# Feed-forward stages of a four-block layer: other priorities and other spans in the planner that sets each engine's order

## What is computed

```python
x = x + _layernorm(attn(_layernorm(x), wq, wk, wv, wo))             # attention, 32 heads
x = x + _layernorm(ffn_lora(_layernorm(x), gate, up, down, a, b))   # silu(gate) * up, then down; 1376 hidden, rank 16
x = x + _layernorm(mixer(_layernorm(x), Win, phz, W1, W2, Wout))    # width 64, 4 layers: complex scan, small MLP
x = x + _layernorm(ffn_int4(_layernorm(x), w1, s1, w2, s2, w3, s3)) # int4 weights with scales, 1376 hidden
```

## Time and profile before

| | us |
|---|---|
| median of 3 runs (838.73 to 839.6) | 838.98 |
| the profiled execution | 840.07 |
| its span, first to last instruction | 838.3 |
| its mean granted clock, full speed being 1 | 0.967 |

### The profile page before, as it was taken

One profiled execution on the slowest core, in us unless ns is written; L12 is line 12 of the kernel. 1 busy time (PEld: TensorE's weight loads), 2 busy tenths in 40 slices (PEclk: granted clock), 3 DMA queues, 4 the chain that ended last, 5 costly groups with the idle time before them and its releaser, 6 DMA issues. The chain is left out here.

```text
span 838.3 us, 12915 instructions
## 1 busy us (share of the span) xinstructions
PE 764.3 (91%) x4483; PEld 555.4 (66%) x4483; DVE 559.1 (67%) x1189; ACT 342.9 (41%) x575; POOL 447.6 (53%) x595
## 2 busy tenths in 40 slices
PE   3999899999988987979998999998989999899995
PEld 2888655555545555758776778775778776578873
DVE  4543677777766369797948787977887977730015
ACT  5111356666666454533333434324443423233510
POOL 4343232443343235754667866847786867474732
PEclk9999899999999998999999999999899999799998
DMA  9002746555470021554673434432154423142301
GB/s 310 7 1 76 236 129 214 177 177 176 158 244 1 1 97 32 179 167 125 192 241 113 135 113 143 132 123 89 39 171 143 119 88 95 38 140 74 91 1 50
DMA packets 56945, 101.38 MB, mean 121 GB/s; under 512 B 13616, under 2 KB 17200, under 8 KB 54704
## 3 DMA queue, kind: packets, MB, share of 16 engines
q1 hardware_dynamic: 53616, 82.21, 31.9%
q0 software_dynamic: 2304, 16.78, 5.5%
q10 hardware_dynamic: 960, 1.57, 0.7%
HBM read 74.58 MB, written 27.00 MB: 121 GB/s over the span
## 5 line engine op out<-in xcount | busy, mean ns | idle before, releaser
L1509 PE MATMUL psum<-xt_hi,wgu_hi 128*128 128x512 f32 (+1 forms) x352 | 142.1, 404 | 2.5 <-POOL wd_lo L783 1.5
L1509 PE MATMUL psum<-xt_hi,wgu_lo 128*128 128x512 f32 (+1 forms) x352 | 142.0, 403 | 0.0
L1509 PE MATMUL psum<-xt_lo,wgu_hi 128*128 128x512 f32 (+1 forms) x352 | 140.5, 399 | 0.0
L783 POOL TENSOR_TENSOR wgu_lo<-raw,wgu_hi 128x512 fp32r<-128x512 f32 (+1 forms) x88 | 116.9, 1332 | 35.7 <-ACT wgu_hi L922 35.2
L1299 DVE TENSOR_REDUCE negmax<-psum 128x2 f32<-128x1024 f32 (+3 forms) x128 | 104.3, 823 | 40.0 <-PE psum L1415 38.9
L820 POOL TENSOR_SCALAR_AFFINE_SELECT probs<-probs 128x256 f32<-128x256 f32 x128 | 52.4, 409 | 121.5 <-ACT probs L979 121.1
L979 ACT ACTIVATE probs<-psum 128x1024 f32<-128x1024 f32 (+3 forms) x128 | 89.6, 710 | 52.2 <-PE psum L1612 50.1
L783 POOL TENSOR_TENSOR wd_lo<-raw,wd_hi 128x512 fp32r<-128x512 f32 (+1 forms) x44 | 59.9, 1370 | 47.6 <-ACT wd_hi L929 47.6
L922 ACT ACTIVATE wgu_hi<-raw 128x512 fp32r<-128x512 f32 (+1 forms) x88 | 54.3, 618 | 73.4 <-PE psum L1506 44.7
L1142 DVE TENSOR_TENSOR hf<-sg,psum 128x512 f32<-128x512 f32 (+1 forms) x44 | 30.1, 683 | 75.2 <-PE psum L1509 63.0
L1529 PE MATMUL psum<-wd_hi,h_hi 128*128 128x512 f32 (+1 forms) x176 | 74.0, 420 | 5.4 <-DVE y L1151 2.9
(11 more groups left out here) (209 smaller groups left out, 1583.8 us busy)
## 6 DMA issues: line engine op xcount, KB each, us to landing
raw<-full SPq DMA_DIRECT2D x60, 256.0 KB, 2.7
raw<-in_gu_t SPq DMA_DIRECT2D x40, 256.0 KB, 2.9
stage_w<-in_w SPq DMA_DIRECT2D x30, 256.0 KB, 2.9
full<-stage_w SPq DMA_DIRECT2D x30, 256.0 KB, 2.8
xt_hi<-turned POOLq DMA_DIRECT2D x7, 1024.0 KB, 5.1
xt_lo<-turned POOLq DMA_DIRECT2D x7, 1024.0 KB, 7.4
turned<-w_hi SPq DMA_DIRECT2D x52, 128.0 KB, 3.1
turned<-w_lo SPq DMA_DIRECT2D x26, 128.0 KB, 2.4
```

What stands on the lines that cost most here:

```text
L783: nc.gpsimd.tensor_tensor(lo, src, hi.bitcast(F32), ALU.subtract).then_inc(sem("w_lo"), 1)
L1509: ins = nc.tensor.matmul(bank[q % 3][0:n, :], (wgu_hi, wgu_lo)[hi_w][:, q % 4, k, 0:n], XT[hi_x][:, k, ch * 512:ch * 512 + 512], start=ite ...
```

## The change

Three things are changed; the instructions stay the same in kind and number, and no value that is computed changes.

1. The planner's choice among events that can begin at the same time. Ranks above 0 no longer count. In their place stands the length of the longest chain of events behind the event, by the planner's spans, plus a constant of the stage that the event belongs to (a table of 17 constants, `URGENT`).
2. The spans given to `put` are new for some 30 kinds of events.
3. The first product of each block and chunk, and `lora_xa`, name all four `xt_lo` tiles of their chunk as what they wait for, where they named the last one; and one of the mixer's two `gate` events names the other.

```diff
-            put("DVE", 1.15, "x_stats", s, tau, ...
+            put("DVE", 1.25, "x_stats", s, tau, ...
-                put("PE", 1.0, "xt", s, tau, ...
+                put("PE", 0.7, "xt", s, tau, ...
-            put("DVE", 1.3, "h_stats", ch, n, k, ...
+            put("DVE", 1.1, "h_stats", ch, n, k, ...
-                    put("DVE", 0.5, "carry", n, ...
+                    put("DVE", 1.4, "carry", n, ...
-                put("PE", 1.0, "wout", tau, ...
+                put("PE", 2.0, "wout", tau, ...
-                put("POOL", 1.3, "w_lo", s, ch, m, c, ...
+                put("POOL", 1.4, "w_lo", s, ch, m, c, ...
-        put("DVE", 0.9, "p_sq", ...
+        put("DVE", 2.8, "p_sq", ...
-            put("DVE", 0.78 if c < 2 else 1.4, "q_shift", m, c, ...
+            put("DVE", 0.85 if c < 2 else 1.7, "q_shift", m, c, ...
-        put("DVE", 0.5, "offsets", 0, ...
+        put("DVE", 2.0, "offsets", 0, ...
...
+        def turned_tiles(s, ch):
+            return [("xt_lo", s, TB * ch + j) for j in range(TB)]
...
-                    start = [("w_lo", s, ch, m, g), ("xt_lo", s - 1, TB * ch + TB - 1), *free] if part == 0 else []
+                    start = [("w_lo", s, ch, m, g), *turned_tiles(s - 1, ch), *free] if part == 0 else []
...
+        URGENT = {('boundary', 0, 0): -57, ('boundary', 0, 1): -81, ..., ('ffn', 3, 0): -308, ('weights', 1, 1): -463, ...}
...
+        while last_ones:
+            e = last_ones.pop()
+            to_end[e] = plan[e][1] + max((plan[e][4] + to_end[f] for f in users[e]), default=0.0)
...
-            e = min(ready, key=lambda e: (max(todo[e][0], idle[plan[e][0]]), todo[e][1], todo[e][2]))
+            e = min(ready, key=lambda e: (max(todo[e][0], idle[plan[e][0]]), min(todo[e][1], 0), -to_end[e] - URGENT.get(part_of(*e), 0), todo[e][2]))
```

More of the change, by code:

```diff
@@ L419, in weights @@
                 put("ACT", 0.65, "w_hi", s, ch, m, c, after=free + [ready], rank=2)
-                put("POOL", 1.3, "w_lo", s, ch, m, c, after=(("w_hi", s, ch, m, c),), rank=2)
+                put("POOL", 1.4, "w_lo", s, ch, m, c, after=(("w_hi", s, ch, m, c),), rank=2)
         def products(s, ch, m):
@@ L519, in sandwich @@
         put("SP", 4.5, "mixer_in", after=(("merged", NM - 1),), lag=4.0)
[L520 removed]
+        put("DVE", 3.2, "scales", after=(("side_lo", 2), ("p_sq",), ("full", 1, 0, 8)), rank=3)
         mixer(0)
@@ L524, in sandwich @@
         ffn(3, 0)
-        put("DVE", 0.5, "offsets", 0, after=[("y_rstd", 2, tau) for tau in range(TB)], rank=1)
-        put("DVE", 0.5, "offsets", 1, after=[("y_rstd", 2, tau) for tau in range(TB, NT)], rank=1)
+        put("DVE", 2.0, "offsets", 0, after=[("y_rstd", 2, tau) for tau in range(TB)], rank=1)
+        put("DVE", 2.5, "offsets", 1, after=[("y_rstd", 2, tau) for tau in range(TB, NT)], rank=1)
         ffn(3, 1)
@@ L540, in sandwich, with part_of @@
                 users[d].append(e)
+        URGENT = {('boundary', 0, 0): -57, ('boundary', 0, 1): -81, ('boundary', 1, 1): -28, ('boundary', 2, 1): 46, ('boundary', 3, 0): 59, ('boundary', 3, 1): -34,
+                  ('dequant', 0, 0): -62, ('ffn', 1, 0): -86, ('ffn', 1, 1): -52, ('ffn', 3, 0): -308, ('mixer', 0, 0): 28, ('mixer', 1, 0): 65,
+                  ('other', 0, 0): -66, ('weights', 1, 0): -241, ('weights', 1, 1): -463, ('weights', 3, 0): -305, ('weights', 3, 1): 51}
+        def part_of(what, *i):
+            if what in ("q_in", "q_shift", "q_scale", "q_keep"):
+                return "dequant", 0, 0
+            if what in ("w_in", "w_hi", "w_lo"):
+                return "weights", i[0], i[1]
+            if what in ("gate_first", "gate_up", "silu", "full", "h_hi", "h_lo", "down"):
+                return "ffn", i[0], i[1]
+            if what in ("y_stats", "y_rstd", "x_sum", "x_stats", "x_rstd", "xn", "xt", "xt_hi", "xt_mix", "xt_lo"):
+                return "boundary", i[0], i[1] // TB
+            if what in ("win", "wout"):
+                return "boundary", 1 + (what == "wout"), i[0] // TB
+            if what in ("part", "sum", "y_full"):
+                return "evict", 0, 0
+            if what in ("merged", "merge", "d_keep", "lora_xa", "lora_xh", "lora_x"):
+                return "lora", 0, 0
+            if what == "carry" or what[0:2] == "p_" or what in ("bout_hi", "bout_lo", "turns", "scales", "decay", "offsets", "out", "mixer_in") or not i or what[0:4] == "side" or what[-2:] == "wo" or what[0:2] == "o_":
+                return "other", 0, 0
+            return "mixer", i[0], 0
@@ L1476, in flow_step @@
                         after(pe, e, "side_lo", k)
-                    after(pe, e, "xt_lo", 0, TB * ch + TB - 1)
+                    for tile in turned_tiles(0, ch):
+                        after(pe, e, *tile)
                     if ch:
@@ L1496, in flow_step @@
                         if m == 0 and g == 0:
-                            after(pe, e, "xt_lo", s - 1, TB * ch + TB - 1)
+                            for tile in turned_tiles(s - 1, ch):
+                                after(pe, e, *tile)
                         if q >= 3:
```

61 lines of the change are left out of this document (33 added, 28 removed).

## The result

The changed kernel takes 818.02 us (median of 4 runs, 816.40 to 821.52) against 838.87; the ratio is 0.9755, with an interval of 0.9723 to 0.9788. The prediction was 819.5, in a range of 810 to 835. The profiled execution took 821.52, the slowest of the four, at a mean clock of 0.975 (the others 0.978 to 0.980).

What follows compares the result with a forecast made beforehand. PE, busy 764.3 of 838.3 us, bounds the kernel, so order pays only where PE waits. Savings of 2.7, 3.6, 2.8, 3.5, 2.0 and 9.2 less 4 make 19.8: 840.07 becomes 820.3, median 819.2; predicted 819.5, range 810 to 835.

Steps and rivals of the forecast that it cites:

- A: Start of ffn(1,0): lora_xa waits less as DVE work ahead of it moves behind; 2.7 us saved, ends 1.5 and 5.5.
- B: Merges in ffn(1,0): two p_low steps go behind merge 4; 3.6 us of 5.65 idle saved, ends 0 and 7.
- C: End of ffn(1,0) and way into mixer 0: h_lo, xt and win come sooner; 2.8 us saved, between 1 and 4.
- D: End of ffn(1,1): y_full ahead of the offsets ends a wait; 3.5 us saved, ends 1 and 6.4.
- E: Way into mixer 1: win, xt and h_turn of tiles 4 to 7 sooner; 2.0 us saved, ends 0 and 2.5.
- F: End of ffn(3,0): down-weight split, wout and xt sooner, half clock open; 9.2 us saved, ends 5 and 10.5.
- G: Both mixers: 84 PE steps stand sooner than their chains may allow; loss of 4 us, ends gain 3, loss 9.
- the rest: From the first product of ffn(3,1) to the last product: same work in the same order, predicted difference 0.
- rival of half the gain: Whole kernel: DVE and POOL lengths change with their neighbours, waits partly return; 10 us gained, 830 (829 median), chance 0.30.
- pot: All that a better order could give: 30.8 us of PE idle and 14.4 of lowered clock, some 45 us.
- the rival: Mixers: PE parks at side steps standing too early, blocking products behind; slower, 846 (844.5 median), chance 0.11.
- signs that the prediction named: Right: short merge waits, earlier y_full and ffn(3,1), no half clock. Wrong: mixer idle over 5 us, or half clock remaining.

Runs made afterwards that it cites:

- h1_first_part: New order up to the start of hidden tile 9 of ffn(1,0), the kernel before's order from there on; 833.59 us, ratio 0.9967.
- fix_d: Changed kernel with xt, xt_hi and xt_lo of s = 2, tile 3, moved sooner at the end of ffn(1,1); 818.05 us, ratio 0.9766.
- light_powers: Changed kernel in its order, with four of six operations of each p_low and p_high step left out; 814.19 us, ratio 0.9724.
- fix_b: Changed kernel with two DVE events moved: p_abs behind the fourth merge, the fifth merge ahead of p_low 0; 816.97 us, ratio 0.9759.
- off_only: Kernel before with one event moved, the first offsets behind the first h_centre of mixer 1; 832.06 us, ratio 0.9947.
- h2_last_part: Kernel before's order up to the start of hidden tile 9 of ffn(3,0), the new order from there on; 828.75 us, ratio 0.9925.
- fix_all: Changed kernel with the moves of fix_d and fix_b, and h_down 1 1 0 one product later; 818.92 us, ratio 0.9784.

## Why the prediction was right, and where it was not

The sum was 820.3 for the profiled execution and 819.2 for the median; the measured values are 821.5 and 818.0. It came so close because errors cancelled: the terms A to F, G and the rest are off by 2.0, 4.1, 1.2, 0.5, 2.0, 1.3, 1.4 and 1.5 us, each way. To that extent the number is luck.

The table of terms is from one execution of either kernel. Traces of other runs have one of the two orders in a stretch and give its distance again; they tell which differences are firm:

| term | old order: before; other traces | new order: after; other traces |
|---|---|---|
| A | 14.2; 14.0, 13.9 | 9.6; 8.9 to 9.5 |
| B | 101.2; 101.1, 101.1 | 101.8; 101.7 (*h1_first_part*), 98.4 (*fix_d*) |
| C | 33.9; 33.9, 33.9 | 32.3; 32.2 to 32.6 |
| D | 16.4; 16.4, 16.4 | 13.4; 13.4, 13.4 |
| E | 19.1; 19.0, 19.0 | 19.2; 19.3 (*light_powers*), 17.1 (*fix_b*) |
| F | 34.4; 34.7, 31.3 (*off_only*) | 23.9; 23.9 to 24.1 |
| G, mixer 0 | 106.7; 106.8, 106.8 | 108.5; 108.3 to 108.4 |
| G, mixer 1 | 87.3; 87.2, 87.3 | 88.2; 88.2 to 89.6 |
| the rest | 93.2; 93.3, 93.7 | 91.7; 91.7 |

A, C, D, G and the rest hold in every trace. B and E of the new order, and F of the old one, depend on the execution.

*F and D* held, in place and in size. F was 10.5 where 9.2 was forecast (7.4 against the trace of *off_only*): the split of hidden tile 10 starts nearly 18 us ahead of its tile's `h_lo` and no longer ends last, the clock stayed at 1.00 (eighth row above), and the new wait at the first product of ffn(3,1) is 0.98 where I had left 1.3. POOL and PE in the changed kernel:

```profile
688.16 1.41 POOL L818 TENSOR_TENSOR wd_lo<-raw,wd_hi 96x512 fp32r<-96x512 f32 x1
705.93 1.29 POOL L823 TENSOR_TENSOR h_lo<-hf,h_hi 96x512 fp32r<-96x512 f32 x1
...
717.82 0.47 PE L1546 MATMUL psum<-xt_hi,wgu_hi 128*128 128x512 f32 x1 [0.98 <-DVE xt_lo L1139]
```

*h2_last_part* shows F alone. D was 3.0 for 3.5: `y_full` came directly behind the `x_sum`, and the new wait that I had put at 2.5 is 3.47 (first row of the section on new waits). *off_only* shows the mechanism alone.

```profile
577.04 1.28 DVE L1186 TENSOR_TENSOR y<-y,psum 128x512 f32<-128x512 f32 x2
```

One price in these sums is a little high. The prediction takes work at half clock as twice as long; in the traces successive products start 0.43 us apart at half clock and 0.23 at full clock, so the 2.97 and 5.12 are rather 2.7 and 4.7, by this estimate.

*B failed.* The step was "Of 5.65 idle I take 3.6 away (the largest wait)". Two `p_low` steps did go behind the merge; but `p_abs` now stands ahead of the merge before it, and two earlier `p_low` steps, the second of them 4.00 long, still stand ahead of this one. So one wait of 3.72 became two, of 2.67 and 2.49, and B lost 0.5. In *fix_d*, with the same order there, the first of them is 1.45, the clock stays up, and B gains 2.8: the forecast's size could be met in some executions, but both waits stand in each of these traces. DVE and POOL around the first of the two waits, in the changed kernel:

```profile
349.52 1.24 DVE L1222 TENSOR_TENSOR low_turn<-chan,pw 128x4 f32<-128x4 f32 x1 [3.12 <-POOL pw L827]
350.69 1.33 DVE L1223 TENSOR_TENSOR low_turn<-chan,pw 128x4 f32<-128x4 f32 x1
352.05 1.20 DVE L1224 TENSOR_TENSOR low_turn<-low_turn,pw 128x4 f32<-128x4 f32 x1
353.28 1.18 DVE L1225 TENSOR_TENSOR pw<-pw 128x4 f32<-128x4 f32 x1
354.50 0.69 DVE L1169 TENSOR_TENSOR raw<-raw,psum 128x512 f32<-128x512 f32 x1
...
349.44 3.79 POOL L818 TENSOR_TENSOR wgu_lo<-raw,wgu_hi 128x512 fp32r<-128x512 f32 x3
353.19 1.26 POOL L818 TENSOR_TENSOR wd_lo<-raw,wd_hi 128x512 fp32r<-128x512 f32 x1
...
355.24 0.50 PE L1525 MATMUL psum<-side_d 128*128 128x512 f32 x1 [2.67 <-DVE raw L1169]
```

Four operations of `p_abs` on 4 elements a partition take 1.18 to 1.33 each, one for each of POOL's four splits, and the last ends as the last split does (354.46 and 354.45). They are the rule that I had weighed: the Trainium skill, "SBUF — State Buffer", section "SBUF: two separate sides", has the shared ports of DVE and GpSimd as an exclusive lock, and this trace agrees with it here as at the earlier trace rows. The offsets show the other direction. Their first three operations took 2.54 at their old place and 0.29 at the new one, between two splits of POOL:

```profile
599.97 0.29 DVE L1132 TENSOR_TENSOR off_tmp<-mv,rstd 128x4 f32<-128x4 f32 x3
...
598.32 1.57 POOL L818 TENSOR_TENSOR wgu_lo<-raw,wgu_hi 128x512 fp32r<-128x512 f32 x1 [2.00 <-ACT wgu_hi L957]
599.85 0.76 POOL L830 TENSOR_TENSOR inv_dev<-var_eps,neghalf 128x2 f32<-128x2 f32 x1
600.58 1.29 POOL L818 TENSOR_TENSOR wd_lo<-raw,wd_hi 128x512 fp32r<-128x512 f32 x1
```

POOL isn't idle there: by the profile `inv_dev`, an operation on 2 elements a partition, runs from 599.85 to 600.61 and doesn't hold the three. In the four traces with moved events or light powers they run within `inv_dev` too, at 0.15 each. So not every POOL operation locks DVE out as these splits do; the lock as it is stated above is too wide here, and the measurement decides. The planner's new span for the event, 2.0, holds at neither place. That the rival of half the gain rested on this and still wasn't the outcome is due to F, more than half of the gain.

*E failed by the clock, not by its waits.* The step was the 2.0 taken for the idle time, with no loss of clock. The idle time of 2.02 went to 0, but the wait at the first product of ffn(3,0) was followed by 3.41 us wholly at half clock:

```profile
583.30:586.72 3.42, 0.15 (x1) 0.18 (x2) 3.42 (x5) 1.09 (x3) 3.26 (x2) 0.75 0.13 32
586.72:590.13 3.41, 3.41 (x9) 2.64 (x10) 3.13 (x9) 0.82 (x1) 2.44 (x9) 0.50 0.41 122
```

The prediction had named this as the low end of D and had not carried it into E. That the clock is the reason shows in *fix_b*, which has the same order here: the wait ahead is 3.5 there too, but the clock stays at 1.00, and E's distance is 2.0 shorter, as forecast. The distance in the changed kernel, and in *fix_b*:

```profile
586.57:605.75 19.18, 19.18 (x97) 16.20 (x98) 14.94 (x44) 9.67 (x16) 14.71 (x25) 0.86 0.42 124
```

```profile
582.88:599.99 17.11, 16.98 (x97) 14.33 (x98) 15.85 (x41) 9.66 (x16) 13.89 (x23) 1.00 0.41 121
```

*A* was larger (4.7 for 2.7), its high end being the half clock, which took less of the first stretch (0.94 for 0.89); also two `xt` fewer stand in this distance than before, one of which is now in B's. *C* was smaller (1.6 for 2.8): the wait of 1.59 for `h_lo` is gone, but PE still waits 1.8 for `xn` there, as it did before (1.7). *The rest* gained 1.5 because the clock is at 1.00 there, where it was 0.98; the prediction had these 1.7 in its pot and in none of its terms.

*G* had the right sign, 2.6 for 4. The one step named, `h_down` directly behind its `up`, waits 0.9 (PE's waits, third line below; the 1.2 in the expectation of *fix_all* isn't in the trace). But in *fix_all*, where it stands one product later, PE waits 2.32 for a `full` ahead of that product, so moving it gained nothing. One reading behind the rival was off: the nine waits of 0.9 in the earlier trace rows are all at `xt`; `win` waited once before the change, for 0.8. PE's waits in the changed kernel beside the earlier trace rows:

```profile
PE psum L1525 <- DVE raw L1169: 5.7, 3, 2.7
PE psum L1493 <- ACT xn L923: 4.9, 5, 2.4
PE psum L1597 <- ACT g L991: 0.9, 1, 0.9
```

Of the signs that the prediction named, `y_full` ahead of the offsets came, and no half clock in the last down phase of ffn(3,0). The first product of ffn(3,1) came 16.9 us sooner, for about 20. "No wait of PE of over 2 us for a merge" did not come (2.67 and 2.49), and one of the signs of being wrong did: the half clock behind a new wait at the first product of ffn(3,0).

What the prediction had not seen at all is how much hangs on the constants. It argued from the finished order, and that was enough for the time; but the words of the change, longest chain and new spans, are the parts that lose 1.9% when they stand without the table.

## What to carry to other kernels

Read the finished order, not the rule that made it: walk each old stall through the new order on the awaited engine, and sum. Where the engine that is waited for works without a gap ahead of the awaited event, count little for a moved event, since in the three kernels here the wait came back at a later one; count it where a single late event holds up the awaited one, as the offsets did. And compare distances between the same two instructions of two traces, not spans or slices, and of more than two traces where others have the same order there.

## What was not expected of the hardware

The half clock is no fixed property of an order. The changed kernel and *fix_d* have the same instructions in the same order up to 560 us. From the first product of ffn(1,0) to hidden tile 4 the one took 30.72 us and the other 27.95; the granted clock of this part was 0.75 in the first over 6.83 us, and 1.00 in the second:

```profile
354.61:361.44 6.83, 6.20 (x22) 4.93 (x23) 4.02 (x8) 1.82 (x5) 2.52 (x2) 0.75 0.69 229
```

```profile
348.00:356.00 8.00, 6.55 (x31) 5.03 (x30) 7.11 (x10) 2.47 (x6) 5.76 (x5) 1.00 0.70 228
```

The same wait of PE in this part, for the fourth merge, was 2.67 in the first execution and 1.45 in the second. E of the changed kernel and of *fix_b* is a second case, behind the same wait. So one order may or may not meet the half clock at a place, and a difference of 2 to 3 us at one place between two traces needs a second look. Also, `wo` of tile 7 started between 318.25 and 321.17 us in the five traces (the changed kernel, the three with moved events, and *light_powers*) that have the same order up to it, a spread as large as most terms.
